# An attention and expert kernel: a chosen order for each pair of slots, new places for the pieces, and two own banks for the tiles' second products

## The reference

```python
mod = (_silu(L0_c) @ L0_wmod).reshape(8, 6, 1, -1)        # sa, ca, ga, sb, cb, gb; |ga|, |gb| at least 0.25
h = _layernorm(x) * (1 + ca) + sa                         # x: 8 sequences x 1024 rows x 256
qkv = h @ w_qkv                                           # 16 heads of 16
scores = einsum('...hqd,...hkd->...hqk', q, k) / 16, causal
x = x + ga * (softmax(scores) @ v @ w_o)
h = _layernorm(x) * (1 + cb) + sb
shared = silu(h @ shared_w1.T) * (h @ shared_w2.T) @ shared_w3.T      # hidden 1024
scores = sigmoid(h @ router_w.T)                          # 8 experts, the two best by scores + bias
routed = sum over the two of gate * ((silu(h1) * h2) @ w3[e].T)       # h1, h2 = h @ w12[e], 256 each
x = x + gb * (shared + routed)
```

## Time and profile before

| | us |
|---|---|
| median of three runs | 2202.41 (2202.2 to 2206.81) |
| the profiled execution | 2220.47 |
| its span, from first to last instruction | 2218.6 |
| TensorE busy in the span | 1999.8 |
| VectorE busy | 1626.2 |
| ScalarE busy | 1067.9 |
| GpSimd busy | 799.4 |

### The profile page before, as it was taken

One profiled execution on the slowest core, in us unless ns is written; L12 is line 12 of the kernel. 1 busy time (PEld: TensorE's weight loads), 2 busy tenths in 40 slices (PEclk: granted clock), 3 DMA queues, 4 the chain that ended last, 5 costly groups with the idle time before them and its releaser, 6 DMA issues.

```text
span 2218.6 us, 47132 instructions
## 1 busy us (share of the span) xinstructions
PE 1999.8 (90%) x17686; PEld 1057.9 (48%) x17686; DVE 1626.2 (73%) x4438; ACT 1067.9 (48%) x1401; POOL 799.4 (36%) x811
## 2 busy tenths in 40 slices
PE   5778889999999899989999999999998988999995
PEld 2223334344444444434443444354444477788773
DVE  6887778776877697768777877787778366655475
ACT  1555544554555455545454545455553545444431
POOL 1110142133223422342234323322323447876653
PEclk8788889998999999999999999899998999999997
DMA  3246220102011201120202020102010446787696
GB/s 124 97 162 200 77 66 22 50 21 71 18 42 38 73 16 49 34 70 16 59 29 65 21 63 26 58 24 60 27 48 21 157 92 114 126 172 121 152 282 203
DMA packets 109661, 175.64 MB, mean 79 GB/s; under 512 B 14576, under 2 KB 80376, under 8 KB 108288
## 3 DMA queue, kind: packets, MB, share of 16 engines
q1 hardware_dynamic: 82848, 136.63, 20.5%
q0 software_dynamic: 26592, 36.00, 8.7%
HBM read 76.43 MB, written 70.44 MB: 66 GB/s over the span
## 4 chain that ended last, share of the span: by engine, by line
PE 60%; DVE 27%; ACT 4%; issue 3%; POOL 3%; DMA 2%; another core or an unknown queue 1%; SPq 1%; POOLq 0%; ACTq 0%; DVEq 0%
PE bank L1794 11%; DVE bank L1247 8%; DVE max_part L1241 8%; PE bank L1846 8%; PE bank L1826 6%; PE bank L1757 5%; PE bank L1709 5%; PE misc L1780 5%; PE bank L1733 4%; PE pv L1780 3%; PE bank L1837 3%; PE bank L1873 2%; PE bank L1719 2%; ACT arena L1050 2%; POOL sum L938 1%
## 5 line engine op out<-in xcount | busy, mean ns | idle before, releaser
L1050 ACT ACTIVATE arena<-bank 128x1024 f32<-128x1024 f32 (+1 forms) x640 | 592.8, 935 | 448.9 <-PE bank L1757 419.9
L1247 DVE CUSTOM_DVE_ANT_0 bank<-bank,mask 128x512 f32<-128x512 f32 (+3 forms) x1024 | 472.2, 520 | 69.1 <-PE bank L1733 58.3
L880 POOL TENSOR_SCALAR_AFFINE_SELECT arena<-arena 128x512 f32<-128x512 f32 x256 | 170.0, 671 | 711.5 <-ACT arena L1050 711.0
L1794 PE MATMUL bank<-feat_parts,ffn_sb 128*128 128x512 f16 x1536 | 371.8, 391 | 7.5 <-ACT arena L1050 3.2
L1241 DVE TENSOR_REDUCE max_part<-bank 128x2 f32<-128x1024 f32 x256 | 312.4, 1220 | 25.8 <-PE bank L1733 23.5
L1757 PE MATMUL bank<-arena 50*128 50x256 f16 (+1 forms) x2560 | 244.7, 271 | 69.7 <-DVE max_part L1241 23.2
L1733 PE MATMUL bank<-arena 48*128 48x512 f16 (+3 forms) x1536 | 233.3, 349 | 57.7 <-DVE max_part L1247 19.4
L938 POOL DMA_INDIRECT sum<-arena,feat x142 | 232.2, 1635 | 136.8 <-DVE arena L1473 65.5
L944 POOL TENSOR_TENSOR hidden<-silu_h,hidden 128x512 f16<-128x512 f32 x128 | 155.8, 1220 | 249.3 <-ACT hidden L1083 248.3
L1780 PE MATMUL misc<-arena,v_sb 128*32 128x256 f32 (+1 forms) x3072 | 236.9, 382 | 1.0 <-POOL arena L880 0.9
L1794 PEld LDWEIGHTS bank<-feat_parts,ffn_sb 128*128 128x128 f16 x1536 | 142.2, 100 | 199.7 <-issue 38.6
(11 more groups left out here) (211 smaller groups left out, 2476.6 us busy)
## 6 DMA issues: line engine op xcount, KB each, us to landing
arena<-parts SPq DMA_DIRECT2D x384, 64.0 KB, 2.2
feat<-lists SPq DMA_DIRECT2D x71, 265.0 KB
sum<-feat_parts SPq DMA_DIRECT2D x9, 1024.0 KB, 6.3
rows<-x SPq DMA_DIRECT2D x8, 1024.0 KB, 5.6
x_sb<-x SPq DMA_DIRECT2D x16, 512.0 KB, 6.5
sum<-norm SPq DMA_DIRECT2D x14, 512.0 KB, 3.3
ffn_parts<-hidden SPq DMA_DIRECT2D x8, 768.0 KB, 4.1
arena<-ffn_parts SPq DMA_DIRECT2D x8, 768.0 KB, 7.0
```

What stands on the lines that cost most here:

```text
L880: gp.affine_select(p, p, [[0, GH], [1, P]], ALU.is_ge, 0.0, 0, -1).then_inc(masked, 1)
L1050: sc.activation(to[:, :, lo:QC], of[:, :, lo:QC], ACT.Exp, scale=SCALE / QK_SCALE ** 2).then_inc(exp_done, 1)
L1247: last = vec.tensor_tensor_reduce(scored, scored, mask[:, 512 - nk:], scale=1.0, scalar=NEG, op0=ALU.add, op1=ALU.max, accum_out=max_part[ ...
L1794: last = mm(to[:, 512 * m:512 * m + 512], w_up[s][W_PART[i]][:, f, m * RH + h * P:m * RH + (h + 1) * P], feat_parts[:, A_PART[i], f, c * 5 ...
```

## The change

Five things change; what is computed is the same.

Inside the slots, the steps of a slot are now five heaps: S (scores), V (values, raw, turn_out, normalise), R (readers), M (the slot's first maximum), U (other pieces and further maxima). Slots are taken in pairs, and a letter for each of the 40 pairs of a sequence names one of eleven orders (ORDERS) of the ten heaps. Sequences 0, 1 and 7 have letters of their own, 2 to 6 share theirs.

The tables have new slots for most pieces, and maxima have slots by MAX_AT. (In the tables of the other sequences, left out here, entries move in the same way.)

Sequences 2 to 6 are still the same steps in the same order, but each is a list with its own name, so each has its own buffers, and no step is tied to a buffer (LAST_USES).

Second products of the tiles (ty) leave the three buffers and go to pv and misc in turn, where they wait for the attention's last steps (tiles 0 and 1) or for the output of the tile two before.

Of END_FFN, 22 items instead of 19 lie between the tiles, the last of them at tile 68; four items (down products) stand behind tile 70, and own(0) comes after the second of them.

```diff
--- before.py
+++ after.py
 TAIL = (
-    (5, "ot", 0), (7, "ot", 1), (11, "op", 0), (12, "rest", 0), (13, "var", 0), (14, "norm2", 0, 0), (15, "norm2", 0, 1), (17, "halves", 0),
-    (18, "ln", 0), (19, "low", 0), (20, "router", 0), (21, "route", 0), (23, "rank", 0), (24, "place", 0), (21, "up", 0), (24, "up", 1),
-    (27, "up", 2), (30, "up", 3), (32, "up", 4), (35, "up", 5), (37, "up", 6), (44, "up", 7), (48, "down", 0), (52, "down", 1), (55, "down", 2),
-    (56, "down", 3), (61, "store", 0), (37, "op", 1), (38, "rest", 1), (47, "var", 1), (51, "norm2", 1, 0), (53, "norm2", 1, 1), (54, "halves", 1),
-    (55, "ln", 1), (56, "low", 1), (66, "router", 1), (72, "route", 1), (73, "rank", 1), (74, "place", 1), (58, "up", 8), (64, "up", 9),
-    (70, "up", 10), (73, "up", 11), (75, "up", 12), (77, "up", 13), (33, "load_x", 1),
+    (7, "ot", 0), (7, "ot", 1), (11, "op", 0), (12, "rest", 0), (13, "var", 0), (15, "norm2", 0, 0), (16, "norm2", 0, 1), (17, "halves", 0),
+    (18, "ln", 0), (19, "low", 0), (20, "router", 0), (21, "route", 0), (22, "rank", 0), (23, "place", 0), (21, "up", 0), (23, "up", 1),
+    (28, "up", 2), (30, "up", 3), (32, "up", 4), (35, "up", 5), (38, "up", 6), (43, "up", 7), (48, "down", 0), (51, "down", 1), (58, "down", 2),
+    (62, "down", 3), (64, "store", 0), (36, "op", 1), (37, "rest", 1), (39, "var", 1), (46, "norm2", 1, 0), (57, "norm2", 1, 1), (61, "halves", 1),
+    (62, "ln", 1), (63, "low", 1), (68, "router", 1), (72, "route", 1), (73, "rank", 1), (74, "place", 1), (64, "up", 8), (66, "up", 9),
+    (70, "up", 10), (73, "up", 11), (75, "up", 12), (78, "up", 13), (32, "load_x", 1),
 )
 SPILL = (
-    (4, "up", -2), (12, "up", -1), (15, "down", -4), (17, "down", -3), (18, "down", -2), (19, "down", -1), (27, "store", -1),
+    (0, "up", -2), (4, "up", -1), (12, "down", -4), (15, "down", -3), (17, "down", -2), (18, "down", -1), (20, "store", -1),
 )
...
 HEAD = (
-    (30, "load_x1"), (33, "spread1", 0), (34, "spread1", 1), (35, "norm1"), (47, "turn", 0), (51, "turn", 1), (54, "qk", 0), (72, "qk", 1),
+    (30, "load_x1"), (34, "spread1", 0), (36, "spread1", 1), (37, "norm1"), (39, "turn", 0), (44, "turn", 1), (47, "qk", 0), (72, "qk", 1),
     (72, "v", 0), (74, "v", 1),
 )
 ALWAYS = (
-    (14, "qk", 2), (34, "qk", 3), (75, "load_x", 0), (70, "load_gates"),
+    (14, "qk", 2), (34, "qk", 3), (75, "load_x", 0), (74, "load_gates"),
 )
 
...
+ORDERS = {
+    "a": "S0 V0 R0 M0 U0 S1 V1 R1 M1 U1", "b": "S0 R0 M0 V0 U0 S1 R1 M1 V1 U1", "c": "S0 R0 M0 V0 V1 S1 M1 U0 R1 U1",
+    "d": "S0 V0 V1 R0 M0 U0 S1 R1 M1 U1", "e": "S0 R0 M0 V0 V1 U0 S1 R1 M1 U1", "f": "S0 V0 R0 U0 M0 S1 V1 R1 U1 M1",
+    "g": "S0 V0 V1 R0 U0 M0 S1 R1 M1 U1", "h": "M0 S0 R0 V0 V1 U0 M1 S1 R1 U1", "i": "S0 V0 R0 M0 U0 S1 R1 M1 V1 U1",
+    "j": "S0 R0 M0 V0 U0 S1 V1 R1 M1 U1", "k": "S0 V0 R0 U0 M0 S1 R1 V1 U1 M1",
+}
+PAIRS_FIRST = "haacjciikkiihiiiiaffeeeebejajjcbiiijcaaa"
+PAIRS_SECOND = "cchcikffifddbbbbbbaabjdijbggbbcebcdakiii"
+PAIRS_LOOP = "jjdbbcjcibbbjbbbbfbkcccakcgdddbcibbbaiaa"
+PAIRS_LAST = "aaibaifcjkbeehcjgbbffffebaidihhhhhhhddbb"
+PAIRS_OF = {"first": PAIRS_FIRST, "second": PAIRS_SECOND, "loop": PAIRS_LOOP, "last": PAIRS_LAST}
 
 
 
...
-LATE_FFN = len(END_FFN) - 7
+LATE_FFN = len(END_FFN) - 4
 FFN_FROM = 52
-FFN_AT = [FFN_FROM + n * (ALL_TILES - FFN_FROM) // LATE_FFN for n in range(LATE_FFN)]
+FFN_AT = [FFN_FROM + n * (ALL_TILES - 2 - FFN_FROM) // LATE_FFN for n in range(LATE_FFN)]
 
 
 OUT_EARLY = 2 * ROUND[0]
 OUT_AT = [SIX_DONE + 2 + m for m in range(OUT_EARLY)]
-MAX_SLOTS = 14
+
+MAX_AT = (0, 1, 2, 3, 3, 4, 5, 6, 7, 8, 8, 9, 10, 10, 11, 11, 13, 13)
+SHIFTS_AT = 14
+MAX_TURN_AT = 16
+ENDS_USE = ("rest", "place", "low", "lengths")
 NORMALISE_AT = 7
 
 
...
@@ -239,50 +254,52 @@
 
     units, tail, spill, head = BODY[v]
     out = []
+    slots = []
     for t in range(SLOTS if units else LAG + 2):
-        if units:
-            out.append(("scores", t))
+        now = {"S": [("scores", t)], "V": [], "R": [], "M": [], "U": []}
+        slots.append(now)
         u = t - LAG
         if (units and u >= 0) or (tail and u < 0):
-            out.append(("values", u))
+            now["V"].append(("values", u))
             if u % SLOTS in STEP_END:
-                out.append(("raw", step_of(u % SLOTS) - (STEPS if u < 0 else 0)))
+                now["V"].append(("raw", step_of(u % SLOTS) - (STEPS if u < 0 else 0)))
         if (u - 1) % SLOTS in STEP_END and ((units and u >= 1) or (tail and u < 1)):
             n = step_of((u - 1) % SLOTS) - (STEPS if u < 1 else 0)
-            out.append(("turn_out", n))
+            now["V"].append(("turn_out", n))
             if n != 0:
-                out.append(("normalise", n))
+                now["V"].append(("normalise", n))
         if not units:
+            out += now["V"]
             continue
         extra = [("normalise", 0)] if t == NORMALISE_AT else []
         for table in TABLES[v]:
             extra += table.get(t, [])
 
-        w = t // GROUP
-        g = (w + 1) % NG
+        g = (t // GROUP + 1) % NG
         s = t % GROUP
-        maxes = []
-        if s < MAX_SLOTS and (g or head):
-            maxes = [("max", g, p) for p in range(MAXES * s // MAX_SLOTS, MAXES * (s + 1) // MAX_SLOTS)]
-
-        readers = ("rest", "place", "low", "lengths")
-        out += [e for e in extra if e[0] in readers]
-        out += maxes[:1]
+        maxes = [("max", g, p) for p in range(MAXES) if MAX_AT[p] == s] if g or head else []
+        now["M"] = maxes[:1]
         for e in extra:
-            if e[0] in PARTS_OF:
+            if e[0] in ENDS_USE:
+                now["R"].append(e)
+            elif e[0] in PARTS_OF:
                 for x in range(PARTS_OF[e[0]]):
-                    out.append((*e, x))
+                    now["U"].append((*e, x))
                     if x == 1:
-                        out += maxes[1:]
+                        now["U"] += maxes[1:]
                         maxes = maxes[:1]
-            elif e[0] not in readers:
-                out.append(e)
-        out += maxes[1:]
+            else:
+                now["U"].append(e)
+        now["U"] += maxes[1:]
         if g or head:
-            if s == MAX_SLOTS:
-                out += [("shifts", g)]
-            if s == MAX_SLOTS + 2:
-                out += [("max_turn", g)]
+            if s == SHIFTS_AT:
+                now["U"].append(("shifts", g))
+            if s == MAX_TURN_AT:
+                now["U"].append(("max_turn", g))
+    if units:
+        for n, name in enumerate(PAIRS_OF[v]):
+            for part in ORDERS[name].split():
+                out += slots[2 * n + int(part[1])][part[0]]
     if not units:
         def put(items):
             for e in items:
@@ -311,7 +328,7 @@
         put([("first_loads",)])
         for n, items in enumerate(END_FFN[LATE_FFN:]):
             put(items)
-            if n == 4:
+            if n == 1:
                 put([("own", 0)])
         put([("own", 1), ("out_end",)])
     return out
...
@@ -320,6 +337,10 @@
 
 BODY = {"first": (True, False, False, True), "second": (True, True, False, True), "loop": (True, True, True, True),
         "last": (True, True, True, False), "end": (False, True, True, False)}
+MIDDLE = ("third", "fourth", "fifth", "sixth", "seventh")
+for v in MIDDLE:
+    BODY[v], TABLES[v], PAIRS_OF[v] = BODY["loop"], TABLES["loop"], PAIRS_OF["loop"]
+del BODY["loop"]
 WORK = {v: work(v) for v in BODY}
 WORK["start"] = [("turn", 0), ("turn", 1), ("qk", 0), ("qk", 1), ("v", 0), ("v", 1)]
 WORK["start"] += [("max", 0, p) for p in range(MAXES)] + [("max_turn", 0)]
@@ -329,13 +350,12 @@
 
 BUFFERS = 3
 BUSY = {"scores": 4, "values": 8, "max": 5, "up": 6, "down": 13, "op": 46, "ot": 14, "ln": 18, "router": 9, "turn": 14,
-        "qk": 46, "v": 46, "turn_out": 5, "max_turn": 8, "rank": 4, "count": 1, "mods": 60, "xr": 9, "tup": 28, "ty": 15}
+        "qk": 46, "v": 46, "turn_out": 5, "max_turn": 8, "rank": 4, "count": 1, "mods": 60, "xr": 9, "tup": 28}
 READ = {"scores": 15, "max": 18, "up": 13, "down": 7, "op": 17, "ot": 15, "ln": 15, "router": 6, "turn": 17,
-        "qk": 30, "v": 17, "max_turn": 14, "rank": 6, "count": 4, "mods": 16, "xr": 18, "tup": 18, "ty": 9}
+        "qk": 30, "v": 17, "max_turn": 14, "rank": 6, "count": 4, "mods": 16, "xr": 18, "tup": 18}
 READ_MASKED = 20
 READER = {"op": "rest", "ln": "low", "rank": "place", "count": "lengths"}
 RINGED = tuple(READ)
-LAST_USES = {("scores", SLOTS - BUFFERS + i): i for i in range(BUFFERS)}
 
 
 def use_of(step):
@@ -355,9 +375,6 @@
         if kind in RINGED and use not in took:
             open_ = [i for i in range(BUFFERS) if owner[i] in closed]
             i = min(open_, key=lambda i: (max(free[i], now), free[i], i))
-            if use in LAST_USES:
-                i = LAST_USES[use]
-                assert i in open_, use
             now = max(now, free[i])
             took[use], after[use], owner[i] = i, (owner[i], owner[i] in took), use
```

(17 more changed lines are left out.)

63 lines of the change are left out of this document (31 added, 32 removed).

## The result

The changed kernel takes 2237.14 us (median of four runs, 2234.33 to 2239.06) beside 2202.3 for the kernel before: 1.0168 times as long, 95% interval 1.0149 to 1.0187. I had forecast 2160.

The account below looks back on a forecast made before the run. TensorE's own time was taken to bound the kernel from sequence 1 on, with VectorE a close second. The terms -17 - 8 - 11 - 7 = -43 us, applied to the median 2202.41, gave 2159.4, say 2160 us, range 2128 to 2192.

Parts of the forecast that it names:

- (a): Inside pairs of slots: 193 fewer changes of TensorE's array use, at 0.096 us each; -17 us (-10 to -18.5).
- (b): TensorE's visible stops in the sequences: moved pieces smooth the load, -1 us per sequence, -8 in all (-40 to +15).
- takes that find their buffer's reader unfinished: Sequences, three shared buffers: such takes stay nearly the same, 37 before and 34 after, 1 us less in all.
- (c): End stage tiles: second products in two banks of their own shorten first products' waits; -11 us (-5 to -14).
- first products find their buffer one and a half tiles old: End stage tiles: first products' buffers were last used one and a half tiles earlier; part of the -11 us.
- banks give nothing: End stage tiles: another chain or the DMA of rows paces them, so separate banks gain nothing; 2171, chance 0.12.
- (d): Kernel's end: last feed-forward pieces move before the last tiles, leaving only down products behind; -7 us (-3 to -10).
- Order gains hidden: Sequences: VectorE or the readers set the pace, so new order and smoothing gain nothing; 2184, chance 0.13.
- Buffers taken too early: Pairs issuing the first maximum before its slot's values lose time on buffers; 2222 at 0.3 us per pair, chance 0.06.
- I am wrong if the span of a middle sequence does not move: Middle sequences: sign against the forecast, which had them take 213 to 216 us instead of 218 to 220.
- The other half of that sign: Kernel's end: forecast is wrong if the last tile's scatter-add is held up by pieces now in front of it.
- The 18 us between profile and timed median: Kernel before: profiled run 2220.47 us, timed median 2202.41; the forecast carried its 43 us gain over unchanged.

Follow-up runs that it names:

- u_b: Kernel before's places and end stage, but every pair of slots has each slot's readers and maxima ahead of its values; 1.0143 to the kernel before.
- u_d: Kernel before's places and end stage, but every pair issues both slots' values together behind the first slot's scores; 1.0300 to the kernel before.
- b_again: The kernel before, unchanged, profiled a second time; ratio 0.9993, timed median 2222.7 us.
- e3_old_end: The kernel after with both end-stage parts undone (second products in the three buffers, seven items behind tile 70); 1.0130 to the kernel before.
- e6_fix: e1_banks, with the planner told that router, rank and count products of the end stage are read much later; 0.9990 to the kernel before.
- e1_banks: The kernel before with one part alone: the tiles' second products go to pv and misc; 1.0018 to the kernel before.
- b_again2: The kernel before, unchanged, profiled on the same chip as three other kernels for comparing stage lengths; 2237.3 us.
- w_before2: The kernel before with VectorE reading half of each maximum product and ScalarE taking exponentials of two of four heads; 0.9377 to the kernel before.
- u_a: Control: places, orders and end stage of the kernel before, made by the kernel after's machinery with its buffer planning; 0.9984 to the kernel before.
- e2_late: The kernel before with one part alone: 22 instead of 19 feed-forward items between the tiles; 1.0007 to the kernel before.

## Why the prediction was wrong, point by point

**(a) Order inside a pair: the saving came, and the time did not follow.** Work in a middle sequence fell by 4.5 to 4.8 us for 24 changes fewer, twice my 2.3, and by 2.5 us for 29 in u_b, 8.0 for 51 in u_d: 0.09 to 0.2 us a change, where I had 0.096. What failed is a condition that the sum never stated and always used: that the stops stay as they are. By the Trainium skill, TensorE: Matmul & The Clock Gate, Single matmul latency, a drain is near 175 ns; order d's 0.16 us is near it, order b's 0.09 is not, and in neither did it decide.

**(b) The stops: -8 us forecast, and they grew.** By my own measure of stops (21.6 and 26.4) it is +4.8 us in each middle sequence where I had -1, as much as (a) saved there, with another 0.5 us of the lower clock level; and in sequence 0 another +3 us, with the lower level held 20 us longer (52 and 72 us), which costs some 10 us there. The +4.8 is of one chip; b_again and e3_old_end give +5.5 by the same measure. Both halves of my argument failed. Adding up VectorE's and TensorE's steps over four slots promised 12 us less and saw nothing of slot 49, where the order within two slots made VectorE idle for 2.04 us and then late by 2.97. And the count of "takes that find their buffer's reader unfinished" (37 and 34) said that it would not get worse: it counts takes by an account of the buffers, not how long each stands.

**(c) Two banks: -11 us forecast, +0.002 by itself.** The named wait did vanish, as I wrote. The step that failed is "first products find their buffer one and a half tiles old". In tiles 10, 14, 15 and 19 they found router's and rank's, 11.4 us of waits in place of the 12.3 that went, with the lower clock level and longer waits for gathered rows on top. Even with that mended in the plan (e6_fix) the gain is 0.1%, within the interval of nothing, and not 0.5%. I had the list of owners before and after within reach and read it for ty only. The rival "banks give nothing" was right about the size; of its two reasons, the DMA of rows is seen in part (2.1 us of waits became 6.0). The Trainium skill, TensorE: Matmul & The Clock Gate, HAM oscillation, tells of a kernel in which double-buffered PSUM gained nothing more; e1_banks and e6_fix agree with that (1.0018, 0.9990), though here by another cause, the inherited buffers.

**(d) Down products ahead: -7 us forecast, 1.0007.** The stop before the last down products is gone and they run in 10.64 us in the kernel after, as I wrote. But I moved the last tile's output by 5.8 us where it moves by 10.5: the low half of the last hidden tile (L1466) took 2.41 us instead of 0.69, since GpSimd's low half (L944), which the change had put there, ran beside it, and TensorE waited 2.73 us for it, and a pair of store operations (2.5 us) came in ahead of the last output on VectorE. Then the reload is waited for (11.80 us), as forecast. Sum: nothing.

**The rivals.** "Order gains hidden" was nearest for the sequences and still too kind. "Buffers taken too early", my one slower rival, belongs to the right family (a take comes before its buffer has been read; 19 stretches of four or more takes with no values between, where there were 6), but names the less costly order: with a maximum ahead of values in all pairs (u_b) the loss is 1.4%, with both values together and no maximum moved (u_d) it is 3.0%, some 67 us over 320 pairs, 0.2 us a pair after what the changes save. My forecast counted "the two V together" only as two changes fewer. And the chance of 0.06 for slower came from one mechanism; the kernel's real exposure was that every saving stood in TensorE's row, while the three buffers made its stops.

**What I had named as signs** read right in hindsight: "I am wrong if the span of a middle sequence does not move": it went from 221.4 to 222.0. The other half of that sign came true as well: the last tile's output, and with it its scatter-add, was 10.5 us late behind the pieces now in front of it. The 18 us between profile and timed median of the kernel before, which I carried over, look like a difference between chips.

## What to carry to other kernels

When TensorE shares a few PSUM buffers with slow readers, products that need no buffer (here the values) can be spacers: count the stretches with more takes in a row than there are buffers, and be wary of gathering the spacers to save changes of the array's use (order d: 1.030). Price any new order as work saved minus stops made, and test the reader's share first by halving one reading; here that was 3.7% and 2.5%, where my price for all the changes saved was 18.5 us, 0.8%. When one user leaves a shared ring, list who inherits each buffer afterwards, for every user, with the time at which the previous one is really read. Before comparing stages of two profiles, look whether both have the same kinds of waits: a kind that one chip shows and another does not can be as large as the effect.

## What the runs showed that I had not expected

Half of VectorE's reading taken away brought 82 us, half of ScalarE's another 56 (by the ratios), in a kernel whose TensorE is busy for 90% of the span. TensorE's busy share in sequence 4 rises only from 93% (209.19 of 224, b_again2) to 98% (196.98 of 200, w_before2), since part of the gain is in busy time itself: the clock was at its lower level for 20.5 us of the first stretch (the most of its middle sequences) and for none of the second.

In sequence 0 the lower clock level goes with the readers: in three profiles of the kernel before it was held 52 to 62 us, with VectorE's reading halved 24 us, and the sequence took 153.8 instead of 172 to 176 us.

The kernel before, unchanged, has medians from 2199 to 2238 us on different chips, a spread of 1.8%, as large as the effect studied here. Ratios within one chip repeat far better (0.9993 for the same kernel again, 0.9984 for its control u_a).

VectorE's low half of a hidden tile (L1466, L1484 after) is held up by GpSimd. In e2_late 66 of its 71 operations have no tensor operation of GpSimd beside them and take at most 0.70 us. The last took 2.41: GpSimd's L944 began 0.12 us after it, took 1.73, and the operation ended 0.56 us after that; 0.69 + 1.73 is 2.42. Two more, of 2.32 and 1.87 us, began while another operation of GpSimd (L950, 2.9 us) was under way, and both ended 0.56 us after its end. (The remaining two stood beside other operations of GpSimd, L884 and L886, and were not longer.) The kernel before has three such too (2.34, 1.88 and 2.00 us in b_again2), but none in front of the last tile's output. So moving a piece of GpSimd's work lengthens VectorE's work beside it, which my sum for (d) left out.
